# Four-bit stage of a two-layer transformer kernel: GpSimd's order within a step, restoring the normalised tile ahead of restoring the gated tile

## The reference, cut to what matters

```python
def fp4_quant_dequant(x):                    # blocks of 16 along the last dim
    scale = max(max(abs(xb)) / 6, 1e-12)
    idx = searchsorted(_MID, abs(xb / scale))
    return _GRID[idx] * sign(xb) * scale
def fp4_linear(x, w):
    return einsum('bsk,nk->bsn', fp4_quant_dequant(x), fp4_quant_dequant(w))
gate, y = fp4_linear(x, w_gate), fp4_linear(x, w_up)
h = silu(gate) * y                           # 704 wide
return fp4_linear(h, w_down)
```

## Time and profile before

| what | us |
|---|---|
| median of 3 runs | 2493.95 |
| lowest and highest run | 2488.51 to 2495.43 |
| profiled execution, its own time | 2493.73 |
| span of the profiled execution | 2492.0 |
| TensorE busy in the span | 2357.8 (95%) |
| VectorE busy | 1785.5 (72%) |
| ScalarE busy | 1292.4 (52%) |
| GpSimd busy | 701.8 (28%) |

### The profile page before, as it was taken

How to read it: one execution, slowest core, us unless ns; L and a number is a source line. 1 busy time by engine, 2 the same in 40 slices (tenths; PEclk the granted TensorE clock), 3 DMA queues, 4 the chain that set the end, 5 groups by cost and what they waited for, 6 DMA issues and landing times.

```text
span 2492.0 us, 43786 instructions
## 1 busy us (share of the span) xinstructions
PE 2357.8 (95%) x16024; PEld 2181.9 (88%) x16024; DVE 1785.5 (72%) x3323; ACT 1292.4 (52%) x2027; POOL 701.8 (28%) x468
## 2 busy tenths in 40 slices
PE   7999995999999969999999999998999999999999
PEld 6999994899999968898988988987988998899998
DVE  5776766899999857566566565565788887877774
ACT  4445543444444325455464464454666765655554
POOL 1110102454444423023023023123334442311110
PEclk9999996999999979999999999996999999999999
DMA  5000000000000000000000000011000010000001
GB/s 183 0 0 0 0 1 20 1 0 0 0 0 1 1 17 1 18 4 13 17 4 13 13 5 16 13 40 51 26 18 25 17 50 28 1 26 26 25 25 34
DMA packets 43259, 45.69 MB, mean 18 GB/s; under 512 B 3120, under 2 KB 41904, under 8 KB 43184
## 3 DMA queue, kind: packets, MB, share of 16 engines
q1 hardware_dynamic: 43184, 44.69, 5.6%
HBM read 27.90 MB, written 16.78 MB: 18 GB/s over the span
## 4 chain that ended last, share of the span: by engine, by line
PE 51%; DVE 6%; issue 3%; ACT 2%; POOL 1%; DVEq 0%; ACTq 0%; POOLq 0%
PE m_ps_z L1848 12%; PE p_ps_a L1630 5%; PE p_ps_feat L279 4%; PE p_ps_a L1687 4%; PE p_ps_feat L281 3%; PE p_ps_feat L280 3%; PE m_ps_wide L279 3%; PE m_ps_wide L281 3%; PE m_ps_wide L280 3%; PE p_ps_a L1568 2%; PE p_ps_turn L1674 2%; PE m_ps_wide L1826 1%; PE m_ps_wide L1827 1%; PE m_ps_n L1809 1%; PE p_ps_b L279 1%
## 5 line engine op out<-in xcount | busy, mean ns | idle before, releaser
L1940 DVE TENSOR_TENSOR m_a_lo<-m_a,m_a_hi 128x512 fp32r<-128x512 f32 x256 | 201.8, 805 | 144.5 <-ACT m_a_hi L1900 141.1
L1848 PE MATMUL m_ps_z<-m_w_hi,m_a_hi 128*128 128x256 f32 x1024 | 290.7, 284 | 1.5 <-DVE m_a_lo L1940 0.9
L1848 PE MATMUL m_ps_z<-m_w_hi,m_a_lo 128*128 128x256 f32 x1024 | 288.0, 281 | 0.0
L1848 PEld LDWEIGHTS m_ps_z<-m_w_hi,m_a_hi 128*128 128x128 f32 x1024 | 192.3, 188 | 13.5 <-DVE d_w_lo L2457 1.8
L1848 PEld LDWEIGHTS m_ps_z<-m_w_hi,m_a_lo 128*128 128x128 f32 x1024 | 192.8, 188 | 0.0
L1896 ACT ACTIVATE m_a<-m_ps_wide,d_b,d_w_gain 128x512 f32<-128x512 f32 x128 | 99.8, 780 | 135.7 <-PE m_ps_wide L281 131.7
L1313 POOL TENSOR_TENSOR p_kf<-p_kf,p_k_shift 128x1024 f32<-128x1024 f32 x64 | 119.4, 1903 | 155.5 <-DVE p_k_shift L1448 155.5
L1848 PE MATMUL m_ps_z<-d_w_lo,m_a_hi 128*128 128x256 f32 x512 | 144.7, 283 | 0.0
L1848 PE MATMUL m_ps_z<-m_w_lo,m_a_hi 128*128 128x256 f32 x512 | 143.6, 280 | 0.0
L1630 PE MATMUL p_ps_a<-p_ctx_pair,p_kf 128*128 128x34 f32 x1024 | 130.1, 285 | 0.0
L1630 PEld LDWEIGHTS p_ps_a<-p_ctx_pair,p_kf 128*128 128x128 f32 x1024 | 129.5, 205 | 0.4
(11 more groups left out here) (350 smaller groups left out, 8019.0 us busy)
## 6 DMA issues: line engine op xcount, KB each, us to landing
residual<-in_x SPq DMA_DIRECT2D x8, 1024.0 KB, 11.8
attn<-p_attn SPq DMA_DIRECT2D x32, 256.0 KB, 2.2
m_attn<-attn SPq DMA_DIRECT2D x16, 512.0 KB, 3.8
out<-residual SPq DMA_DIRECT2D x16, 512.0 KB, 2.9
raw_weights<-in_d_q SPq DMA_DIRECT2D x2, 1024.0 KB, 7.2
m_attn<-in_d_scale SPq DMA_DIRECT2D x3, 512.0 KB, 4.1
raw_weights<-in_m_w1T SPq DMA_DIRECT2D x1, 1024.0 KB, 5.0
raw_weights<-in_m_w2T SPq DMA_DIRECT2D x1, 1024.0 KB, 8.4
```

The costliest lines, as they stand in the source:

```text
L1848: mm = pe.matmul(z, a, w[:, f, :], start=(f == 0 and k == 0 and j % 2 == 0), stop=(f == FC - 1 and k == 2), skip_group_check=True)
L1940: dve.tensor_tensor(self.a2[1][:, f, :], self.a[f % RING][:, :], self.a2[0][:, f, :].bitcast(F32), ALU.subtract).then_inc(self.a_lo, 1)
```

## The change

The second and the third phase of GpSimd's step change places. Nothing else is edited: the same instructions, with the same operands, semaphores and lags.

```diff
-            pipeline(pool, N, [(6, divide_h), (6, restore_h), (3, restore_n), (2, divide_n)], SLOTS)
+            pipeline(pool, N, [(6, divide_h), (3, restore_n), (6, restore_h), (2, divide_n)], SLOTS)
```

## The result

The changed kernel takes 2512.04 us (median of 5 runs, 2505.37 to 2512.51) against 2493.95 (5 runs, 2488.51 to 2495.43). The ratio is 1.0071, 95% interval [1.0057, 1.0085], that is 14 to 21 us more. The forecast was 2507.7, range 2499 to 2514.

A forecast was written before the change was run, and what follows sets the result against it. TensorE's circle was taken to bound the four-bit stage, VectorE's a quarter of a microsecond behind. 8 x 0.44 + 18 x 0.56 = 13.6 us, with two end steps 14; 2493.73 + 14.0 = 2507.7 us, range 2499 to 2514.

The forecast's parts named there:

- Two circles: Dependency loops of a four-bit step, gated dividing to next: one through TensorE, bounding; one through VectorE, a quarter microsecond behind.
- The moved restoring at 641.00: GpSimd's restoring of the normalised tile begins after its rounding, ends at 642.06, and getting it sooner gains nothing.
- the normalised dividing: GpSimd's dividing of the next normalised tile could move only from 648.07 to about 647.6; worth 0.
- GpSimd first by 0.09 us: GpSimd's restoring begins at 641.00, VectorE's gated rounding L199 at 641.09; L199 is held up and ends 0.83 us later.
- VectorE first in one step in three: L199 begins 0.05 us ahead; the restoring runs between L199 and L201, and L201 pays up to 0.89 us.
- Every order costs VectorE about the same.: GpSimd first, VectorE first, or VectorE keeping both turns with restorings and L182 some 0.9 us later: 0.83 for all.
- The room ahead of multiply 1: VectorE's idle time before its second multiplication, 0.54 us, less the gap after a reciprocal: 0.39 outside the loop, 0.27 inside.
- The sum: 8 steps at 0.44 us, 18 in the loop at 0.56, two end steps at 0.2 each: together 14 us.
- The signs: Expected in the profile: L199 about 2.45 us, steps 15.3 to 15.4, idle before multiply 1 0.15 to 0.3, TensorE waiting over 1.2.
- Cover that holds: Rival: VectorE's idle time ahead of multiply 1 hides the collision; not slower, 2494 us; 10 in 100.
- shared bandwidth: Rival: VectorE runs at half speed beside GpSimd, costing 0.53 us a collision; 5.8 us in all, 2499.5; 7 in 100.
- The one with both circles pushed: Rival: lock held longer or twice, or TensorE's up 1 delayed too; a microsecond a step, 26 us, 2520; 7 in 100.

The follow-up runs named there:

- the second comparison: The changed kernel measured once more, unchanged, against the kernel before on another occasion: 2509.25 us against 2494.16, ratio 1.0055 [1.0041, 1.0068].

## Why the prediction was right

- **Two circles, TensorE's last by a quarter of a microsecond.** Right: freed of its wait, the stage gained 0.25 us a step.
- **The moved restoring at 641.00 and done in 1.06 us, the normalised dividing worth nothing.** Right: 1.35 us behind the gated dividing's end; nobody who waited before waits for either.
- **GpSimd first by 0.09 us and L199 0.83 late; VectorE first in one step in three, L201 late, up to 0.89.** Right in kind and number: 2.45 us, 0.83 more; 2.37 on L201, 0.75 more. The upper bound for that order was too high, because the restoring's 1.06 was counted in full behind L199's end at 667.37; it ended 0.92 behind that, at 668.29.
- **"Every order costs VectorE about the same."** Half right. The two orders that occur cost 0.83 and 0.75. The third, which I put in with them, costs 0.29 us a step more.
- **The room ahead of multiply 1, 0.39 us outside the loop and 0.27 inside.** Mis-sized by 0.06 in both, in two parts. What VectorE needs behind the reciprocal was taken from the additions, 0.15 outside and 0.27 inside; ahead of multiply 1 it is 0.26 and 0.34. The idle time of before was taken from one step, 0.54; it is 0.54 to 0.57 in nearly all steps of the loop, up to 0.62 outside. The first row is of before, outside the loop, the second of after:

```profile
811.58 0.89 DVE L957 TENSOR_TENSOR f_h_q<-f_ps_up,f_silu 128x704 f32<-128x704 f32 x1 [0.60 <-PE f_ps_up L281]
```
```profile
472.89 0.89 DVE L957 TENSOR_TENSOR f_h_q<-f_ps_up,f_silu 128x704 f32<-128x704 f32 x1 [0.26 <-DVE f_n_inv L185]
```

That leaves some 0.33 us of room outside and 0.21 inside. The 8 steps outside cost 3.8 us instead of 3.5, and the 18 inside 10.5 instead of 10.1, although six of these pay only the 0.75 of L201. Two steps at the ends cost 0.4 and 0.2 us, where the prediction has 0.2 each. Together that is the 1 us by which the stage exceeds the forecast.

- **The sum.** 14.0 us forecast, 15.0 in the stage. The median's further 3 us (18.1) are not in the stage in either execution of the changed kernel, and the second comparison has a difference of 15.1.
- **The signs.** The restoring 1.35 us behind the dividing, L199 and L201 and the releaser of multiply 1 came as named. The idle time ahead of multiply 1 is 0.34 us in the loop, just over the 0.3 named. TensorE waiting over 1.2 us a step is met only if both of its waits are counted: 1.1 for silu and 0.2 for the first multiplication. The steps are 15.37 us outside the loop and 15.43 on the average inside, at the upper edge of 15.3 to 15.4.
- **The rivals.** Cover that holds, shared bandwidth: out, by 2.45 us of L199. The one with both circles pushed: TensorE's up 1 does wait, and its first matmul begins at 655.34, 6.50 us after the dividing's end at 648.84, against 6.27 before; that is 0.23 late and stays behind VectorE's own way, which is 0.6 late.

## What to carry to other kernels

When an instruction is moved into idle time, ask what runs beside it there and not only what waits for it: 1.06 us of GpSimd reading SBUF were free beside a VectorE instruction with an operand in PSUM, and cost 0.83 us beside one with both in SBUF. Moving it past that one doesn't have to help either: put off until the rounding was over, it pushed the next restoring onto L182 and cost 0.84 us a step. Idle time of the second-busiest engine at one place is the room that any delay must fit into, and it is less than it looks by what the engine needs between two dependent instructions anyway. A wait of the busiest engine is worth only what the next circle leaves: 0.86 us of TensorE's waiting brought 0.25.

## What the runs showed of the hardware

- Semaphores are not the only thing that makes one engine wait for another: VectorE's L199 stood still for 0.83 us beside GpSimd's multiplication of a spare tile that nobody reads and that no semaphore ties to it.
- Starts 0.09 us apart decide who is served, and do so the same way every time: in both executions of the changed kernel L199 of the gated tile lasts 2.44 to 2.45 us wherever GpSimd is first. It ends 1.47 to 1.49 us behind GpSimd's instruction, that is its own 1.62 less 0.14.
- The engine that waits is served as soon as the other's instruction ends, even if that engine has its next one 0.04 us later: the restoring got in between L199, which ended at 667.37, and L201, which began at 667.41 and waited.
- One input tile alone doesn't keep VectorE clear of GpSimd: behind the held-back restoring L182 (128x32) took 1.51 us instead of 0.18, while the reduction L180 (128x512 to 128x32) kept its 0.68 beside the same instruction.
- A memset of GpSimd over 128 x 1024, 0.95 us, costs a two-input instruction of VectorE nothing.
